# A Swin block and a dilated-convolution block on one core: the pyramid's matmuls spread evenly over four column tiles and reordered, the edge gate summed as rows and spread by a transfer

## The chip, the cores and the metric

The kernel runs on one core of one Trainium2 chip. The metric is the device time of one execution in microseconds (us); lower is better. All data are float32. An "image" below is one of 16 inputs of 128 channels by 32 x 32 points, held as 128 partitions x 1024 elements.

## The reference, cut to what matters

Two blocks follow each other for each image. The first is a Swin block (layer norm, attention in windows of 8 x 8 points with 8 heads, projection, layer norm, an MLP of 512 hidden channels). The second is a convolution block; the part of it that the change touches is this:

```python
out0 = gelu(conv2d(x, in_w, in_b))
feats = [conv2d(out0, pyr_w[i], pyr_b[i], pad=(d, d), dil=(d, d), groups=dim // 4)
         for i, d in enumerate((1, 6, 12, 20))]          # 3 x 3 taps, 32 outputs each
pyr = conv2d(conv2d(concatenate(feats), fuse_w, fuse_b, groups=dim), cr_w[2], cr_b[2], pad=(1, 1), groups=dim)
edge = sigmoid(conv2d(out0, vis_w, vis_b, pad=(1, 1)))   # one plane for all channels
out = x + cw0 * (1 + edge) * h_out + cw1 * (1 + edge) * v_out + cw2 * (1 - 0.3 * edge) * pyr + cw3 * point + cw4 * x_sca
```

`h_out` and `v_out` are dilated convolutions along one axis followed by 3 x 3 ones, and `x_sca` goes through a 2-D Fourier transform, a product and the inverse transform. Relu and a last 1 x 1 convolution close the block.

## The kernel before, in words

**Order of the work.** Each engine has a hand-written list of steps, and semaphores join them. The convolution block of image n runs beside the Swin block of image n + 1, in a function `both(n, i)` that every engine has; the queues run it 15 times, and `conv_only` handles the last image. Within `both` a front stretch (input convolution, layer norm, keys, queries, values) is followed by eight slots j = 0 to 7, one for each pair of attention windows, and then by a tail (projection, MLP, output convolution). In slot j TensorE issues `scores(j + 2)`, `conv_early(n, j)`, `prob_transposes(j)`, `conv_late(n, j)` and `values(j)`. VectorE does `bias_max(j + 2)` (L957 and L960), `row_sums(j)` (L964 and L966) and `conv_slot(n, j)`. GpSimd subtracts the maxima (`less_max`, L1666), and ScalarE takes the exponents (`exponent`, L1382) and copies the transposed probabilities (`prob_copy`, L1387). An engine works its list in order, so a step that waits holds up everything behind it.

**The front stretch on TensorE** is: `in_conv` (L607), `x_transposes`, `edge_products` (L628), two taps of the pyramid's first half, `gap_products` (L614, L615), five more taps, `n_transposes` (L459, which waits for the normalised rows `nT` of VectorE, L929), `mid_products` (L620, L621), `queries_keys` (L489, L494), `v` (L504), the last two taps, then `scores(0)` and `scores(1)` (L518). These two wait for `spread_keys` (L428), eight transfers that the SP queue issues once VectorE has written the keys `kC` (L949). Taps 0 to 4 of the pyramid's second half come behind the two scores, tap 5 in slot 0, and taps 6 to 8 in slot 1.

**The pyramid** (`pyramid`, L674) computes the four dilated 3 x 3 convolutions. The image's rows are split in two halves k of 16 rows; half k goes to PSUM bank 4 + k. Dilation d (1, 6, 12, 20) owns column tile d of the array, that is 32 output partitions, so up to four matmuls can run side by side, each with 128 rows and 32 columns. A tap reads a shifted rectangle, and points outside the image are left out. So tile 0 (dilation 1) takes 4,418 columns in each half, tile 1 takes 3,528, tile 2 takes 2,592 and tile 3 takes 1,568. In the profile each float32 matmul is two instructions. The second half waits for `route_z` and `xs_sb`, two signals of `scaled_input` on VectorE. ScalarE copies each half to `pyr` (`pyr_copy`, L1452), and `stack_pyramid` on the SP queue (L417) makes three shifted copies of it in `pyr_stack` with 12 transfers; `pyramid_conv` (L647, slot 5) reads them.

**The edge gate.** `edge_products` yields nine planes, one for each tap of the 3 x 3 filter. `spread_edge` on the SP queue writes them to DRAM and reads them back shifted, as nine partitions (`z_run`, L410). In slot 5, TensorE adds the nine and spreads the sum over all 128 partitions by a matmul with ones (`edge_spread`, L637, 2 x 512 columns, into banks 6 and 7), ScalarE takes two tanh of 128 x 512 (`edge_tanh`, L1437) and then the gate of the pyramid (`edge_cuts`, L1445), which VectorE's `gate_pyramid` (L1139, slot 6) waits for. `inverse_even` (slot 5, in the same banks, the first L467 group after VectorE's `even_product` L1117) waits for the tanh, and ScalarE's `inverse_even_copy` stands behind `edge_cuts` in its list.

**The Fourier part** goes back and forth between TensorE and ScalarE: `x2_conv` (slot 1), `dft_rows` and `turn_spectrum` (slot 2), `r_even` and `dft_columns` (slot 3), `r_odd` (slot 4). VectorE mirrors the input in slot 1 (`odd_part`), adds a bias in slot 3 (`r_even_bias`, L1099), boosts in slot 4 (`boosted`, L1108) and multiplies in slot 5. VectorE's share of the axis convolutions is 18 passes of 128 x 1024 (`taps`, L1088 and L1090); nine of them run in the tail, ahead of `gate_axes` (L1147), `add_magnitude` (L1153) and `mixture` (L1159), on which ScalarE's relu (L1521) and the output convolution (L755) wait.

## Time and profile before

| what | us |
|---|---|
| three runs, median (lowest, highest) | 1809.78 (1808.87, 1812.44) |
| the profiled execution, its own time | 1805.41 |
| span of the profiled execution | 1803.6 |
| TensorE, busy | 1549.4 |
| VectorE, busy | 1364.0 |
| ScalarE, busy | 864.2 |
| GpSimd, busy | 684.9 |

The span is one execution on the core as the profiler saw it, and what lies around it (1.8 us) is launch and end. Busy times are summed over the instructions of an engine, and they overlap between engines. TensorE is busiest by this count, but its matmuls are pipelined, and a busy engine need not be the one that sets the end; which one does is read from the chain of waits and from the timelines. The mean granted clock of TensorE is 0.953 of full speed.

### The profile page before, as it was taken

The page shows a single profiled execution, that of the slowest core. Times are in us where ns is not written, and L with a number is a line of the kernel's source. Part 1 is how long each engine was busy: PE and PEld are TensorE (multiplying, and loading weights), DVE is VectorE, ACT ScalarE, POOL GpSimd, SP SyncE. Part 2 cuts the span into 40 slices and gives each one's busy share as a digit, 9 for nine tenths or more (in the row PEclk, how much of TensorE's full clock was granted, in tenths as well). Part 3 has the DMA queues.
Part 4 walks back from the last instruction along what each step waited for, and adds up shares of the span by engine and source line. Part 5 has one row for each costly group of instructions (what it writes and reads, how often), then busy time and mean ns, then how long its engine had stood idle before and what let it go on. Part 6 is the DMA issues. An engine that isn't in the chain of part 4 may idle for free.

```text
span 1803.6 us, 32142 instructions
## 1 busy us (share of the span) xinstructions
PE 1549.4 (86%) x11664; PEld 906.3 (50%) x11664; DVE 1364.0 (76%) x2455; ACT 864.2 (48%) x1380; POOL 684.9 (38%) x603
## 2 busy tenths in 40 slices
PE   5789899888989889888998988889888898988884
PEld 3346455464555546445463554546455464555542
DVE  4558778687777878788687777868788786778866
ACT  2344545455454544545455454544545545454533
POOL 3244251634416244251534416134251623416151
PEclk9899999999999999999999999999999999999997
DMA  4011020111102011020111102011020201102020
GB/s 147 1 26 41 26 52 1 43 33 37 39 23 53 0 37 39 25 51 0 43 33 37 39 23 53 0 37 39 25 51 0 58 18 37 39 12 53 0 54 12
DMA packets 19618, 60.23 MB, mean 33 GB/s; under 512 B 6228, under 2 KB 6228, under 8 KB 19204
## 3 DMA queue, kind: packets, MB, share of 16 engines
q1 hardware_dynamic: 19588, 59.83, 13.7%
q8 instruction: 18, 0.29, 0.1%
q14 instruction: 12, 0.10, 0.0%
HBM read 14.04 MB, written 9.02 MB: 13 GB/s over the span
## 4 chain that ended last, share of the span: by engine, by line
DVE 39%; PE 25%; DVEq 16%; issue 7%; ACT 6%; SPq 4%; DMA 3%; ACTq 1%; POOL 0%; POOLq 0%
DVE hv L1090 16%; DVEq L959 7%; DVE nT L929 5%; PE bank L647 5%; PE bank L674 4%; SPq L428 4%; DVE row_max L960 4%; DVEq L965 3%; PE bank L467 3%; PE bank L518 3%; PE bank L489 2%; DMA k_heads<-kC 2%; PE bank L755 2%; DVE score L957 2%; PE bank L577 1%
## 5 line engine op out<-in xcount | busy, mean ns | idle before, releaser
L674 PE MATMUL bank<-act,mats_sb 128*32 128x512 f32 (+11 forms) x2112 | 267.1, 475 | 1.4 <-DVE xs L1026 1.4
L1666 POOL TENSOR_TENSOR score<-score,row_max 128x512 f32<-128x512 f32 x128 | 133.4, 1042 | 306.7 <-DVE row_max L960 305.1
L1350 ACT ACTIVATE fft<-bank 128x512 f32<-128x512 f32 x224 | 168.9, 807 | 125.7 <-PE bank L467 111.8
L1090 DVE SCALAR_TENSOR_TENSOR hv<-hor,mix,hv 128x1024 f32<-128x1024 f32 x128 | 193.8, 1514 | 10.7
L467 PE MATMUL bank<-cons_sb,fft 128*128 128x128 f32 x1280 | 185.4, 306 | 11.8 <-DVE fft L1117 11.8
L1090 DVE SCALAR_TENSOR_TENSOR hv<-ver,mix,hv 128x1024 f32<-128x1024 f32 x144 | 186.9, 1298 | 11.0
L1382 ACT ACTIVATE score<-score 128x512 f32<-128x512 f32 x128 | 80.8, 631 | 225.8 <-POOL score L1666 225.8
L467 PEld LDWEIGHTS bank<-cons_sb,fft 128*128 128x128 f32 x1280 | 172.7, 217 | 31.4 <-DVE fft L1117 17.0
L1677 POOL COPY inv_wide<-row_inv 128x128 f32<-128x128 f32 x128 | 91.8, 717 | 206.7 <-DVE row_inv L966 206.7
L674 PEld LDWEIGHTS bank<-act,mats_sb 128*32 128x32 f32 x2112 | 117.5, 109 | 99.6 <-issue 81.5
L1696 POOL TENSOR_SCALAR hor<-act,cols_sb 128x1024 f32<-128x1024 f32 x16 | 18.0, 1125 | 391.6 <-ACT act L1407 391.6
L518 PE MATMUL bank<-k_heads,qC 128*64 128x512 f32 x512 | 136.1, 621 | 31.8 <-DMA k_heads<-kC 31.8
L577 PE MATMUL bank<-nC,mats_sb 128*128 128x512 f32 x256 | 127.4, 621 | 38.9 <-ACT nC L1350 23.4
L957 DVE TENSOR_TENSOR score<-bank,rel_bias 128x512 f32<-128x512 f32 x128 | 87.2, 681 | 76.3 <-PE bank L518 76.2
L1387 ACT ACTIVATE probT<-bank 128x512 f32<-128x512 f32 x128 | 77.7, 607 | 101.6 <-PE bank L529 101.3
L1706 POOL TENSOR_SCALAR axis_part<-act,cols_sb 128x320 f32<-128x320 f32 (+1 forms) x128 | 109.4, 855 | 22.5 <-issue 22.5
L587 PE MATMUL bank<-fft,mats_sb 128*128 128x512 f32 x256 | 115.2, 593 | 0.0
L1400 ACT ACTIVATE fft<-bank,fold_b 128x512 f32<-128x512 f32 x128 | 79.2, 689 | 68.5 <-PE bank L577 68.5
L929 DVE TENSOR_SCALAR nT<-xT,mv,rstd 128x128 f32<-128x128 f32 x256 | 104.8, 491 | 3.8
L1708 POOL TENSOR_TENSOR ver<-ver,axis_part 128x320 f32<-128x320 f32 (+1 forms) x64 | 100.8, 1575 | 9.4
L960 DVE TENSOR_REDUCE row_max<-score 128x8 f32<-128x512 f32 x128 | 87.8, 686 | 11.6
L577 PEld LDWEIGHTS bank<-nC,mats_sb 128*128 128x128 f32 x256 | 45.1, 191 | 98.2 <-issue 34.4
(180 smaller groups left out, 2903.9 us busy)
## 6 DMA issues: line engine op xcount, KB each, us to landing
pyr_stack<-pyr SPq DMA_DIRECT2D x192, 144.2 KB, 3.1
x_in<-x_dram SPq DMA_DIRECT2D x16, 512.0 KB, 3.5
k_heads<-kC SPq DMA_DIRECT2D x128, 64.0 KB, 2.4
out_dram<-y_out SPq DMA_DIRECT2D x16, 512.0 KB, 2.8
k_heads<-rel_dram SPq DMA_DIRECT2D x2, 1024.0 KB, 13.0
mats_sb<-mats_dram SPq DMA_DIRECT2D x1, 1978.5 KB, 7.4
z_dram<-z_sb SPq DMA_DIRECT2D x32, 19.1 KB
z_run<-z_dram SPq DMA_DIRECT2D x16, 38.2 KB
```

The costliest lines, as they stand in the source:

```text
L467: last = pe.matmul(dst[:, c * P:(c + 1) * P], src[:, at:at + P], rhs, start=True, stop=True)
L518: last = pe.matmul(bank[2 + j % 2][64 * e:64 * e + 64, :], qC[:, w * WT:(w + 1) * WT], k_heads[:, :, w], start=True, stop=True)
L577: pe.matmul(bank[b][:], w_up[:, f * P:(f + 1) * P], nC[:, HALF * k:HALF * k + HALF], start=True, stop=True).then_inc(up_ps, 1)
L587: last = pe.matmul(bank[b][:], w_down[:, f * P:(f + 1) * P], hidden[:, f, HALF * k:HALF * k + HALF], start=False, stop=(f == FC - 1))
L674: last = pe.matmul(grids[32 * d:32 * d + 32, y0 - 16 * k:y1 - 16 * k, x0:x1], w_pyr[:, d, t], act[:, y0 + dy:y1 + dy, x0 + dx:x1 + dx], st ...
L929: last = dve.tensor_scalar(nT[:, c], source[:, c], mv[:, c, 0:1], rstd[:, c:c + 1], ALU.subtract, ALU.mult)
L957: dve.tensor_tensor(score[:, j % 3].rearrange("p h k -> p (h k)"), bank[2 + j % 2][:], rel_bias[:], ALU.add).then_inc(s_biased, 1)
L959: dve.drain()
L960: dve.tensor_reduce(row_max[:, j % 3], score[:, j % 3], AX.X, ALU.max).then_inc(s_max, 1)
L1090: last = dve.scalar_tensor_tensor(hv[:], src, mix[:, a, k:k + 1], hv[:], ALU.mult, ALU.add)
L1350: return act_.activation(dst, src, ACT.Copy)
L1666: pool.tensor_tensor(score[:, j % 3], score[:, j % 3], row_max[:, j % 3].unsqueeze(2).broadcast_to([P, HEADS, WT]), ALU.subtract)\
```

## The change: what it does

Five things change. The pyramid's dilation 1 keeps 12 rows of each half in tile 0; the other 8 rows of the image (24 to 31) go to tile 3, into partitions 96 to 127 of bank 7. A half then takes at most 3,528 columns in one tile: the tiles hold 3,290, 3,528, 2,592 and 2,696 columns in the first half and 3,384, 3,528, 2,592 and 2,602 in the second, in 42 matmuls each where there were 33. `pyramid_pieces` orders them by the columns that each tile has had so far. ScalarE gets a third copy (`rest_copy`, slot 1, ahead of the second `pyr_copy`), `stack_pyramid` issues 18 transfers, and the second half of `x2_conv` waits for the new copy, since it overwrites bank 7.

The second half no longer waits for `route_z` and `xs_sb`, and the taps are placed otherwise: three of the first half, `gap_products`, the other six and two of the second half ahead of `n_transposes`; three of the second half ahead of `scores(0)`; none behind `scores(1)`. Tap 5 and taps 6 to 8 stay in slots 0 and 1.

The edge planes are read back as rows (`z_rows`, 32 partitions, one for each row of the image) with three transfers; VectorE sums them in slot 1 (`sum_edge`, 32 x 32 out of 32 x 288); ScalarE takes one tanh of 32 x 32 in slot 2; and `widen_edge` on the SP queue, behind `stack_pyramid`, writes the 4 KB to DRAM and reads them into all 128 partitions. The matmul `edge_spread` is gone, `edge_cuts` and `gate_axes` wait for the transfer, and `inverse_even` waits for `boosted` in place of the tanh.

```diff
-                taps = bass.AP(z_dram, 0, [[3 * GRID1 + S1, 3], [GRID1 + 1, 3], [1, RUN]])
-                sp.dma_start(z_run[0:9, 0:RUN], taps).then_inc(z_in, 16)
+                for y in range(3):
+                    taps = bass.AP(z_dram, y * (3 * GRID1 + S1), [[S1, SIDE], [GRID1 + 1, 3], [1, SIDE]])
+                    sp.dma_start(z_rows[0:SIDE, 3 * y:3 * y + 3], taps).then_inc(z_in, 16)
+            def widen_edge(n):
+                sp.wait_ge(edge_tanhed, n + 1)
+                sp.dma_start(edge_dram[:], edge_rows[0:SIDE]).then_inc(edge_out, 16)
+                sp.wait_ge(edge_out, 16 * n + 16)
+                sp.dma_start(edge.rearrange("p h w -> p (h w)"), bass.AP(edge_dram, 0, [[0, P], [1, TOK]]))\
+                  .then_inc(edge_sb, 16)
             def stack_pyramid(n):
                 sp.wait_ge(pyr_sb, 2 * n + 2)
+                sp.wait_ge(rest_sb, n + 1)
+                flat = pyr.rearrange("p h w -> p (h w)")
+                rest = pyr_rest.rearrange("p h w -> p (h w)")
+                end = 33 * S1 + SIDE
+                low, high = (1 + MAIN1) * S1, (1 + 2 * MAIN1) * S1
                 for s in range(3):
-                    for j in range(4):
-                        src = pyr[32 * j:32 * j + 32].rearrange("p h w -> p (h w)")
-                        sp.dma_start(pyr_stack[32 * s:32 * s + 32, j, 0:33 * S1 + SIDE], src[:, s:s + 33 * S1 + SIDE])\
+                    part = slice(32 * s, 32 * s + 32)
+                    for j in range(1, 4):
+                        sp.dma_start(pyr_stack[part, j, 0:end], flat[32 * j:32 * j + 32, s:s + end])\
                           .then_inc(pyr_stacked, 16)
+                    sp.dma_start(pyr_stack[part, 0, 0:low - s], flat[0:32, s:low]).then_inc(pyr_stacked, 16)
+                    sp.dma_start(pyr_stack[part, 0, low - s:high - s], flat[0:32, 17 * S1:17 * S1 + high - low])\
+                      .then_inc(pyr_stacked, 16)
+                    sp.dma_start(pyr_stack[part, 0, high - s:end], rest[96:P, 0:end - high + s])\
+                      .then_inc(pyr_stacked, 16)
...
                 stack_pyramid(n)
+                widen_edge(n)
                 store(n)
...
                 return max(first, -off), min(first + count, SIDE - off)
+            def pyramid_pieces(k):
+                chains = [[(0, MAIN1 * k, MAIN1, t) for t in PYR_ORDER]]
+                chains += [[(d, 16 * k, 16, t) for t in PYR_ORDER] for d in range(1, 4)]
+                chains[3] += [(0, 2 * MAIN1 + REST1 // 2 * k, REST1 // 2, t) for t in PYR_ORDER]
+                pieces, busy = [], [0, 0, 0, 0]
+                while any(chains):
+                    tile = min((g for g in range(4) if chains[g]), key=lambda g: busy[g])
+                    d, first, count, t = chains[tile].pop(0)
+                    (y0, y1) = inside(first, count, (t // 3 - 1) * DILS[d])
+                    (x0, x1) = inside(0, SIDE, (t % 3 - 1) * DILS[d])
+                    if y1 > y0:
+                        pieces.append((tile, d, first, t, y0, y1, x0, x1, not chains[tile]))
+                        busy[tile] += max(64, (y1 - y0) * (x1 - x0))
+                return pieces
+            PYR_PIECES = [pyramid_pieces(k) for k in range(2)]
             def pyramid(n, k, steps):
                 pe.wait_ge(act_sb, 2 * n + 2)
                 if k == 0:
                     pe.wait_ge(out_sb, 2 * n)
-                else:
-                    pe.wait_ge(route_z, n + 1)
-                    pe.wait_ge(xs_sb, n + 1)
+                pieces = PYR_PIECES[k]
                 grids = bank[4 + k].rearrange("p (h w) -> p h w", w=SIDE)
-                for step in steps:
-                    t = PYR_ORDER[step]
-                    for d, dil in reversed(tuple(enumerate(DILS))):
-                        dy, dx = (t // 3 - 1) * dil, (t % 3 - 1) * dil
-                        (y0, y1), (x0, x1) = inside(16 * k, 16, dy), inside(0, SIDE, dx)
-                        if y1 > y0:
-                            last = pe.matmul(grids[32 * d:32 * d + 32, y0 - 16 * k:y1 - 16 * k, x0:x1], w_pyr[:, d, t],
-                                             act[:, y0 + dy:y1 + dy, x0 + dx:x1 + dx],
-                                             start=(step == 0), stop=(step == 8), skip_group_check=True)
-                    if step == 8:
+                rest = bank[7].rearrange("p (h w) -> p h w", w=SIDE)
+                for at in range(len(pieces) * steps[0] // 9, len(pieces) * (steps[-1] + 1) // 9):
+                    tile, d, first, t, y0, y1, x0, x1, final = pieces[at]
+                    dy, dx = (t // 3 - 1) * DILS[d], (t % 3 - 1) * DILS[d]
+                    if tile == d:
+                        to = grids[32 * d:32 * d + 32, y0 - first:y1 - first, x0:x1]
+                    else:
+                        to = rest[96:P, y0 - 2 * MAIN1:y1 - 2 * MAIN1, x0:x1]
+                    last = pe.matmul(to, w_pyr[:, d, t], act[:, y0 + dy:y1 + dy, x0 + dx:x1 + dx], start=(t == 4),
+                                     stop=(t == PYR_ORDER[8]), skip_group_check=True)
+                    if final:
                         last.then_inc(pyr_ps, 1)
...
                     pe.wait_ge(xs_sb, n + 1)
+                    if k == 1:
+                        pe.wait_ge(rest_sb, n + 1)
...
                     pe.wait_ge(ge_sb, n + 1)
-                    pe.wait_ge(edge_sb, 2 * n + k + 1)
+                    pe.wait_ge(w_sb, 2 * n + 2)
...
-                elif j == 5:
-                    edge_spread(n)
...
                 in_conv(n)
                 x_transposes(i)
                 edge_products(n)
-                pyramid(n, 0, range(0, 2))
+                pyramid(n, 0, range(0, 3))
                 gap_products(n)
-                pyramid(n, 0, range(2, 7))
+                pyramid(n, 0, range(3, 9))
+                pyramid(n, 1, range(0, 2))
                 n_transposes(i)
                 mid_products(n)
                 queries_keys(i)
                 v(i)
-                pyramid(n, 0, range(7, 9))
+                pyramid(n, 1, range(2, 5))
                 scores(i, 0)
                 scores(i, 1)
-                pyramid(n, 1, range(0, 5))
                 for j in range(PAIRS):
                     if j + 2 < PAIRS:
...
+            def sum_edge(n):
+                dve.wait_ge(z_in, 48 * n + 48)
+                dve.wait_ge(edge_tanhed, n)
+                dve.tensor_reduce(edge_sum[0:SIDE], z_rows[0:SIDE].rearrange("p t x -> p x t"), AX.X, ALU.add)\
+                   .then_inc(edge_summed, 1)
...
                 elif j == 1:
+                    sum_edge(n)
                     odd_part(n)
...
             def edge_tanh(n):
-                for k in range(2):
-                    act_.wait_ge(eb_ps, 2 * n + k + 1)
-                    act_.wait_ge(gated_sb, n)
-                    act_.activation(edge[:, 16 * k:16 * k + 16], bank[6 + k].rearrange("p (h w) -> p h w", w=SIDE),
-                                    ACT.Tanh, bias=half_vis_b[:], scale=0.5).then_inc(edge_sb, 1)
+                act_.wait_ge(edge_summed, n + 1)
+                act_.wait_ge(edge_out, 16 * n)
+                act_.activation(edge_rows[0:SIDE], edge_sum[0:SIDE], ACT.Tanh, bias=half_vis_b[0:SIDE], scale=0.5)\
+                    .then_inc(edge_tanhed, 1)
             def edge_cuts(n):
-                act_.drain()
+                act_.wait_ge(edge_sb, 16 * n + 16)
                 act_.wait_ge(axis_sb, 2 * n + 2)
                 act_.wait_ge(cw_sb, n + 1)
                 act_.activation(edge_cut[:], edge[:], ACT.Identity, bias=mix[:, 2, 1:2], scale=mix[:, 2, 0:1])\
                     .then_inc(cut_sb, 1)
             def pyr_copy(n, k):
-                act_.wait_ge(pyr_ps, 2 * n + k + 1)
-                act_.wait_ge(pyr_stacked, 16 * 12 * n)
+                act_.wait_ge(pyr_ps, 8 * n + 4 * k + 4)
+                act_.wait_ge(pyr_stacked, 16 * 18 * n)
                 act_.activation(pyr[:, 1 + 16 * k:17 + 16 * k, 1:1 + SIDE],
                                 bank[4 + k].rearrange("p (h w) -> p h w", w=SIDE), ACT.Identity, bias=fuse_bias[:],
                                 scale=col("fuse_w")).then_inc(pyr_sb, 1)
+            def rest_copy(n):
+                act_.wait_ge(pyr_ps, 8 * n + 8)
+                act_.wait_ge(pyr_stacked, 16 * 18 * n)
+                act_.activation(pyr_rest[96:P, 0:REST1, 1:1 + SIDE],
+                                bank[7][96:P, 0:REST1 * SIDE].rearrange("p (h w) -> p h w", w=SIDE), ACT.Identity,
+                                bias=rest_bias[96:P], scale=col("rest_w")[96:P]).then_inc(rest_sb, 1)
...
                 elif j == 2:
+                    edge_tanh(n)
                     row_spectrum_copy(n)
-                elif j == 5:
-                    edge_tanh(n)
...
             def conv_late(n, j):
                 if j == 1:
+                    rest_copy(n)
                     pyr_copy(n, 1)
                     x2_copy(n)
```

## Rows read from the trace of the kernel before

**Rows 1.** The page: busy time of PE, and the engines' shares of the chain.

```profile
PE 1549.4 (86%) x11664; PEld 906.3 (50%) x11664; DVE 1364.0 (76%) x2455; ACT 864.2 (48%) x1380; POOL 684.9 (38%) x603
...
DVE 39%; PE 25%; DVEq 16%; issue 7%; ACT 6%; SPq 4%; DMA 3%; ACTq 1%; POOL 0%; POOLq 0%
```

**Rows 2.** Timeline of PE, one image: start us, us, instructions, [idle before it <-releaser].

```profile
968.32 1.88 PE L607 MATMUL bank<-xm,mats_sb 128*128 128x512 f32 x4
...
974.81 4.27 PE L674 MATMUL bank<-act,mats_sb 128*32 128x480 f32 x34
...
981.54 0.66 PE L459 MATMUL bank<-cons_sb,nT 128*128 128x128 f32 x4 [1.80 <-DVE nT L929]
...
988.20 1.87 PE L674 MATMUL bank<-act,mats_sb 128*32 128x144 f32 x16
992.20 1.94 PE L518 MATMUL bank<-k_heads,qC 128*64 128x512 f32 x8 [2.13 <-DMA k_heads<-kC]
994.07 4.42 PE L674 MATMUL bank<-act,mats_sb 128*32 128x512 f32 x40
...
1002.16 2.62 PE L674 MATMUL bank<-act,mats_sb 128*32 128x128 f32 x20
...
1013.06 1.08 PE L518 MATMUL bank<-k_heads,qC 128*64 128x512 f32 x4
```

**Rows 3.** Timeline of DVE, same image and columns.

```profile
999.54 0.69 DVE L957 TENSOR_TENSOR score<-bank,rel_bias 128x512 f32<-128x512 f32 x1 [2.13 <-PE bank L518]
...
1001.80 0.11 DVE L1064 TENSOR_REDUCE vec<-route 128x1 f32<-128x5 f32 x1
...
1015.64 0.68 DVE L957 TENSOR_TENSOR score<-bank,rel_bias 128x512 f32<-128x512 f32 x1
...
1023.25 0.68 DVE L964 TENSOR_REDUCE row_sum<-score 128x8 f32<-128x512 f32 x1
...
1028.11 1.34 DVE L1117 TENSOR_TENSOR fft<-fft 128x1024 f32<-128x1024 f32 x1
...
1038.41 0.75 DVE L1139 SCALAR_TENSOR_TENSOR py<-bank,cols_sb,axis_part 128x512 f32<-128x512 f32 x1 [1.73 <-PE bank L647]
```

**Rows 4.** Timeline of ACT, same image and columns.

```profile
988.29 0.21 ACT L1427 ACTIVATE route<-route 128x5 f32<-128x5 f32 x1
...
1000.12 0.60 ACT L1387 ACTIVATE probT<-bank 128x512 f32<-128x512 f32 x1
...
1029.23 1.24 ACT L1445 ACTIVATE axis_part<-edge,mix 128x1024 f32<-128x1024 f32 x1
```

**Rows 5.** Timeline of PE around slot 5, same image and columns as Rows 2.

```profile
1025.90 1.97 PE L637 MATMUL bank<-z_run,ones 9*128 9x512 f32 x4 [0.99 <-DVE fft L1113]
...
1029.50 3.55 PE L467 MATMUL bank<-cons_sb,fft 128*128 128x128 f32 x16 [1.04 <-DVE fft L1117]
```

**Rows 6.** Timeline of SP, same image: the first issue's start, us, issues.

```profile
1006.69 7.50 SPq L417 DMA_DIRECT2D pyr_stack<-pyr  x12
```

**Rows 7.** The page, DMA issues: count, KB each, median us from issue to landing.

```profile
x_in<-x_dram SPq DMA_DIRECT2D x16, 512.0 KB, 3.5
...
k_heads<-rel_dram SPq DMA_DIRECT2D x2, 1024.0 KB, 13.0
```

**Rows 8.** Timeline of PE, where later images' in_conv begins, same columns.

```profile
1074.99 0.59 PE L607 MATMUL bank<-xm,mats_sb 128*128 128x512 f32 x1
...
1182.89 1.45 PE L607 MATMUL bank<-xm,mats_sb 128*128 128x512 f32 x3
...
1292.57 1.88 PE L607 MATMUL bank<-xm,mats_sb 128*128 128x512 f32 x4
...
1399.23 1.88 PE L607 MATMUL bank<-xm,mats_sb 128*128 128x512 f32 x4
```

**Rows 9.** Windows: from:to us, us, busy (x) by engine, PEclk, DMA share, GB/s.

```profile
1029.40:1036.20 6.80, 6.70 (x48) 4.43 (x52) 3.69 (x7) 3.65 (x4) 0.49 (x2) 0.76 0.00 0
...
1196.60:1203.40 6.80, 6.80 (x13) 3.42 (x12) 2.72 (x5) 0.94 (x2) 6.17 (x7) 0.50 0.02 2
```

More of the change, by code:

```diff
@@ L48 @@
 GRID1 = S1 * S1
-RUN = 31 * S1 + SIDE
+MAIN1 = 12
+REST1 = SIDE - 2 * MAIN1
 AXIS_DIL, AXIS_TAPS = 11, 7
@@ L315, in swin_conv_kernel @@
         z_in = sem("z_in")
-        eb_ps = sem("eb_ps")
+        edge_summed = sem("edge_summed")
+        edge_tanhed = sem("edge_tanhed")
+        edge_out = sem("edge_out")
         edge_sb = sem("edge_sb")
@@ L319, in swin_conv_kernel @@
         pyr_sb = sem("pyr_sb")
+        rest_sb = sem("rest_sb")
         pyr_stacked = sem("pyr_stacked")
@@ L445, in _ @@
             stack_pyramid(IMAGES - 2)
+            widen_edge(IMAGES - 2)
             store(IMAGES - 2)
@@ L448, in _ @@
             stack_pyramid(IMAGES - 1)
+            widen_edge(IMAGES - 1)
             store(IMAGES - 1)
@@ L630, in edge_products @@
                 last.then_inc(z_ps, 1)
-            def edge_spread(n):
-                pe.wait_ge(w_sb, 2 * n + 2)
-                pe.wait_ge(z_in, 16 * n + 16)
-                for k in range(2):
-                    pe.matmul(bank[6 + k][:], ones[0:9], z_grid[0:9, 16 * k:16 * k + 16, 0:SIDE], start=True,
-                              stop=True).then_inc(eb_ps, 1)
             def pyramid_conv(n):
                 pe.wait_ge(go_sb, 2 * n + 2)
-                pe.wait_ge(pyr_stacked, 16 * 12 * n + 16 * 12)
+                pe.wait_ge(pyr_stacked, 16 * 18 * n + 16 * 18)
                 for k in range(2):
@@ L1284, in _ @@
             dve.tensor_scalar(fuse_bias[:], col("pyr_b"), col("fuse_w"), col("fuse_b"), ALU.mult, ALU.add)
+            dve.tensor_scalar(rest_bias[:], col("rest_pyr_b"), col("rest_w"), col("rest_b"), ALU.mult, ALU.add)
             dve.tensor_scalar(two_b1[:], row("fgm_b1"), 2.0, None, ALU.mult)
@@ L1433, in edge_tanh @@
             def edge_tanh(n):
-                for k in range(2):
-                    act_.wait_ge(eb_ps, 2 * n + k + 1)
-                    act_.wait_ge(gated_sb, n)
-                    act_.activation(edge[:, 16 * k:16 * k + 16], bank[6 + k].rearrange("p (h w) -> p h w", w=SIDE),
-                                    ACT.Tanh, bias=half_vis_b[:], scale=0.5).then_inc(edge_sb, 1)
+                act_.wait_ge(edge_summed, n + 1)
+                act_.wait_ge(edge_out, 16 * n)
+                act_.activation(edge_rows[0:SIDE], edge_sum[0:SIDE], ACT.Tanh, bias=half_vis_b[0:SIDE], scale=0.5)\
+                    .then_inc(edge_tanhed, 1)
             def edge_cuts(n):
-                act_.drain()
+                act_.wait_ge(edge_sb, 16 * n + 16)
                 act_.wait_ge(axis_sb, 2 * n + 2)
@@ L1641, in _ @@
             pool.sem_inc(z_zeroed, 1)
-            for padded in (hor, ver, pyr):
+            for padded in (hor, ver, pyr, pyr_rest):
                 pool.memset(padded[:], 0.0)
@@ L1798 @@
     put("pyr_b", conv["pyr_b"].reshape(-1))
+    for name, of in (("rest_w", "fuse_w"), ("rest_pyr_b", "pyr_b"), ("rest_b", "fuse_b")):
+        cols[96:P, COLS[name][0]] = conv[of].reshape(-1)[:32]
     put("vis_b", np.repeat(conv["vis_b"], P))
```

12 lines of the change are left out of this document (8 added, 4 removed).

## The prediction

> **What bounds the kernel now.** I read the page first, then the chain, then the timelines of one image. The page puts PE at 1549.4 us of busy time, but the chain that ended last lies on DVE and its queue for 55% and on PE for 25% [rows 1]: DVE sets the end, and PE counts where DVE waits for it. The timelines say where. In the image from 968.32 to 1074.99, DVE has one long wait for PE ahead of the slots, 2.13 us at 999.54 [rows 2, 3]. PE was running five taps of the pyramid's second half then (4.42 us from 994.07), with the scores that DVE wanted queued behind them [rows 2]. DVE then runs almost without a gap to `even_product` at 1028.11, waits in slot 6 for `pyramid_conv` (1.73 us for the second half, which begins at 1038.41), and is busy again to the tail's end [rows 3]. PE has holes of its own: 1.80 us before the second `n_transposes` and 2.13 us before `scores(0)`, where it waits for the transfer of the keys [rows 2].
>
> **Cost of a column.** The 20 matmuls of 994.07 load tile 0 most, with 2,512 columns. At 1.667 ns a column (four cycles of 2.4 GHz) that is 4.19 us, and 0.23 us of start and end give the 4.42 of the row. The three taps at 1002.16 (1,441 columns in tile 0) give 2.40 + 0.22 = 2.62, again the row [rows 2]. So a stretch of pyramid costs the columns of its fullest tile, and the other tiles run free beside it.
>
> A rule of the Trainium skill speaks against this: TensorE: Matmul & The Clock Gate, Part 3 (The mechanism), says that matmuls start and end strictly in program order. Started so, each when its tile is free and the one before it has begun, the 20 matmuls would take 7.2 us by my count from their columns. The row has 4.42, so this trace does not agree; by the row the sum below is 1789, by the rule it would be the last but one of the rivals, 1889.
>
> **The change, part by part, in that image.**
>
> 1. *Ahead of `n_transposes`.* Before, seven taps load tile 0 with 3,426 columns. Afterwards three taps (1,120 in the fullest tile), `gap_products`, and the other six with two of the second half (3,364, tile 1) make 4,484: 1,058 more, 1.76 us. The hole behind the first transposes is 1.80 us [rows 2], so this just fits, at no cost. `gap_products` comes 143 columns (0.24 us) later, and DVE still waits for ScalarE's standard deviation after it: nothing. Were that cover short, each tenth of a us here would move the keys and everything behind them.
> 2. *Ahead of `scores(0)`.* Three taps with 1,152 columns take 1.92 + 0.22 = 2.14 us, where 1.87 stood; the hole of 2.13 behind them takes the 0.27 [rows 2]. Cost nothing. The two old waits are long met there.
> 3. *Behind `scores(1)`.* The 4.42 us go. `scores(2)` can start when bank 2 is read, at about 994.1, and is done 1.08 later [rows 2]. DVE is free at 999.54 - 2.13 = 997.41, so its wait shrinks to about 0.07: **2.06 us** earlier [rows 3]. From here PE idles until ScalarE's `prob_copy(0)` at 1000.12, which waits for DVE, GpSimd and the exponent and does not move [rows 4].
> 4. *Slot 1.* The last taps cost 1,256 columns, 2.31 us, for 2.62 [rows 2]. But `x2_conv`'s second half waits for `rest_copy`, which ScalarE begins after `prob_copy(1)`. Its cost lies between a copy of 128x5 (0.21) and one of 128x512 (0.60) [rows 4]; I take 0.45 for 32x256. This gives back the 0.3, so `scores(5)` ends where it did, 1013.06 + 1.08 = 1014.14 [rows 2].
> 5. *`sum_edge` on DVE.* 288 elements a partition, between the reduction of five (0.11) and of 512 (0.68) [rows 3]: 0.4. `z_in` is long there: SP issues the three reads well before the keys. The small tanh on ScalarE in slot 2 costs about 0.21 [rows 4] and is over before `dft_rows` has a result for it to copy: nothing.
> 6. *What is late next.* DVE would begin `bias_max(5)` 2.06 - 0.4 = 1.66 us earlier than 1015.64 [rows 3], at 1013.98, and finds the scores done at 1014.14 and a signal behind them: 1014.24, a gain of **1.4 us**. The chain behind it (`r_even_bias`, `r_odd`, `scores(7)`, `boosted`) hangs on DVE, and `even_product` comes 1.4 us earlier. PE's work from there to the tail is unchanged, so PE and DVE both move by 1.4.
> 7. *`edge_spread` gone.* 1.97 us of PE [rows 5], in a stretch where PE waits for `even_product` anyway (1.04 more behind it): nothing gained, and the wait before `inverse_even` grows to over 3 us.
> 8. *The edge transfer.* SP starts `stack_pyramid` where it did (1006.69). 18 issues at 7.50 / 12 = 0.63 us end at 1018.0 [rows 6]. Then 0.63 and about 2.5 for the 4 KB (under the 3.5 that 512 KB need), 0.63 and 3.5 for the 512 KB [rows 7] put `edge` there at 1025.3. ScalarE comes to `edge_cuts` at about 1029.23 - 1.4 - 1.97 = 1025.9 [rows 4, 5], needs 1.24 for it, and must then be free for `inverse_even`'s first copy near 1029. Cost nothing, with 2 us in hand. The stacked copies land by about 1021.5, long before `pyramid_conv`. Behind them SP has only the store, which waits for the image's end.
>
> **The clock.** Images come in a cycle of three: 107.90, 109.68 and 106.66 us [rows 8]. In the 109.68 one the granted clock is 0.50, half of 2.4 GHz, from 1196.6 to 1203.4, just behind the 1.8 us hole and across keys and queries [rows 9]. That image is 1.8 us longer than its neighbour, and there are five such among 15. The new taps fill the hole, so I take this drop as gone: -9. In every image the clock also falls before `inverse_even` (0.76 over 1029.4 to 1036.2 [rows 9]); its 16 instructions take 3.55 us [rows 5]. The idle time ahead of it grows, and I add 0.2 us an image: +3. And the new idle stretch from 995.3 to 1000.8, broken by one group of transposes and one tap, lies before taps, `x2_conv` and `scores(5)`. A drop there would cost PE half of some 3 us and eat the 1.4: I count it for a third of the images, +7.
>
> **Sum.** 15 x 1.4 = 21; the last image gains 1 (its pyramid runs 1.5 us shorter ahead of `mid_products`, less `sum_edge`), and the larger setup nothing that shows. -21 - 1 - 9 + 3 + 7 = -21 us: 1805.4 for the profiled execution's own time becomes 1784.4. The median of the runs is 4.4 us above that execution, so I forecast 1784.4 + 4.4 = **1789** (-1.2%). A measurement can tell 0.2%, about 3.6 us.
>
> **The rivals.**
>
> - *The clock holds too.* No new drop, and the copy's wait shorter so that DVE keeps 1.66: -25 - 1 - 9 + 0 = -35, 1775. For it: one short stretch of work breaks the idle time. Chance 0.12.
> - *The clock falls in the emptied stretch in most images (no change).* For it: the idle time is longer than the hole that preceded the drop at 1196.6 [rows 9]. A drop of 3.3 us (0.76 over 6.8 us is half clock for that long) costs PE 1.7 before `scores(5)`, 0.3 more than the gain: +4.5 - 9 + 3 - 1, about 1807. Chance 0.12.
> - *Slower: the same drop, twice as long, every image.* The drop at 1196.6 lasted 6.8 us [rows 9]; 3.4 us lost ahead of `scores(5)` is 2.0 beyond the gain. It decides from the point where `scores(5)` ends over 1.4 us later. 15 x 2.0 - 9 + 3 - 1 = +23, 1833. Against it: PE works solidly from 1000.8 on. Chance 0.08.
> - *The edge is late.* Two broadcasts of 1 MB took 13.0 us each [rows 7]. At 13 us `edge` lands at 1035, ScalarE holds `inverse_even`'s copies until then, but `turn_even` wants them only near 1040, and `gate_pyramid` loses some 0.8 us: +12, 1801. Chance 0.06.
> - *Program order.* If the tiles did wait for one another, the uneven pieces ahead of `n_transposes` would take 14.2 us, 6.7 more than summed, and 15 x 5.3 us would make it about 1889. That is the skill's rule of above. The trace bears it out nowhere. Chance 0.02.
> - *The forecast's own case*, 1778 to 1800: chance 0.60.
>
> **How the numbers follow.** Faster by over 0.2%: 0.60 + 0.12 + 0.06 and 0.03 of the case at 1807, that is 0.81. Within 0.2%: the rest of that case less its upper edge, 0.08. Slower: 0.11. The range 1772 to 1807 leaves out the slower cases and half of the one at 1807.
>
> **What would show it.** Right: no wait of DVE for L518 before `bias_max(2)`; the pyramid's busy time down by 14 to 20%; images of some 105.5 us with no clock of 0.50 in the keys. Step 6 is wrong if DVE waits more than 0.3 us at `bias_max(5)`, step 1 if `n_transposes` starts late without waiting for DVE, step 8 if ScalarE waits over 3 us for the transfer. The forecast falls if the granted clock is 0.50 between slots 0 and 2 in most images.

## The result and the profile after

The changed kernel takes 1827.07 us (median of four runs, 1826.86 to 1828.2). The kernel before took 1811.11 us beside it (four runs, 1808.87 to 1814.13). The ratio on record is 1.0074, 95% interval 1.0047 to 1.0101 (the two medians alone give 1.0088): slower, where 1789 was forecast with a range to 1807. The profiled execution took 1827.1 us (span 1825.3). Before's took 1805.4, less than any of its four runs, so the two traces differ by 21.7 us of span and the medians by 16. The mean granted clock fell from 0.953 to 0.928.

From the page after: busy time of the engines (PE is TensorE, PEld its weight loads, DVE VectorE, ACT ScalarE, POOL GpSimd), the shares of the chain, the pyramid's group, and the edge's transfer. Beside it stands [rows 1]; the last line is the pyramid's group on the page before.

```profile
PE 1507.9 (83%) x12176; PEld 928.0 (51%) x12176; DVE 1368.7 (75%) x2472; ACT 847.3 (46%) x1380; POOL 702.2 (38%) x604
...
DVE 39%; PE 28%; ACT 9%; DVEq 8%; issue 8%; SPq 4%; DMA 3%; POOL 1%; ACTq 1%; POOLq 0%
...
L712 PE MATMUL bank<-act,mats_sb 128*32 128x512 f32 (+13 forms) x2688 | 243.0, 436 | 0.0
...
edge<-edge_dram SPq DMA_DIRECT2D x16, 512.0 KB, 3.6
```

```profile
L674 PE MATMUL bank<-act,mats_sb 128*32 128x512 f32 (+11 forms) x2112 | 267.1, 475 | 1.4 <-DVE xs L1026 1.4
```

PE is busy 41.5 us less than before, and the kernel is slower. So the time is not in the amount of work. The pyramid's busy time fell by 9%, where 14 to 20% were forecast; part of its taps now run at half speed, as shown below.

Where the images begin says which part of the program it is in. By line, `in_conv` after: duration least/median/most, first and last start.

```profile
L636 PE MATMUL bank<-xm,mats_sb x64: 592/592/697, 107.8 to 1747.7; 128*128 128x512 f32 x64
```

The same line before:

```profile
L607 PE MATMUL bank<-xm,mats_sb x64: 592/592/697, 101.9 to 1724.8; 128*128 128x512 f32 x64
```

First to last start is 1639.9 us after and 1622.9 before, **+17.0**. The last start is that of the sixteenth image's fourth instruction, 1.3 us behind its first, in both; so fifteen images take (1639.9 - 1.3) / 15 = 109.2 us each instead of 108.1. Ahead of the first image it is 107.8 for 101.9, **+5.9**. The last image takes 1825.3 - 1746.4 = 78.9 for 80.1, **-1.2**. Together 21.7.

PE's timeline of the image from 1091.12 to 1200.32; it answers to [rows 2, 5].

```profile
1091.12 1.88 PE L636 MATMUL bank<-xm,mats_sb 128*128 128x512 f32 x4
...
1097.81 5.89 PE L712 MATMUL bank<-act,mats_sb 128*32 128x341 f32 x71
1103.62 1.40 PE L488 MATMUL bank<-cons_sb,nT 128*128 128x128 f32 x8
...
1111.02 2.13 PE L712 MATMUL bank<-act,mats_sb 128*32 128x384 f32 x28
1114.96 2.95 PE L547 MATMUL bank<-k_heads,qC 128*64 128x512 f32 x12 [1.80 <-DMA k_heads<-kC]
1119.49 0.65 PE L558 MATMUL bank<-cons_sb,score 128*128 128x128 f32 x4 [1.58 <-ACT score L1428]
1120.08 0.89 PE L712 MATMUL bank<-act,mats_sb 128*32 128x416 f32 x10
1123.39 0.66 PE L569 MATMUL bank<-probT,v_pair 128*32 128x64 f32 x16 [2.43 <-ACT probT L1433]
1123.98 1.98 PE L547 MATMUL bank<-k_heads,qC 128*64 128x512 f32 x4
1125.89 3.62 PE L712 MATMUL bank<-act,mats_sb 128*32 128x124 f32 x28
...
1131.45 1.13 PE L496 MATMUL bank<-mats_sb,xs 128*128 128x128 f32 x8 [0.47 <-ACT pyr_rest L1506]
...
1138.48 1.08 PE L547 MATMUL bank<-k_heads,qC 128*64 128x512 f32 x4
...
1153.47 3.78 PE L496 MATMUL bank<-cons_sb,fft 128*128 128x128 f32 x16 [4.00 <-DVE fft L1161]
1157.18 6.30 PE L668 MATMUL bank<-pyr_stack,mats_sb 96*32 96x512 f32 x48
```

The front is as the steps wanted it: both `n_transposes` in one go at 1103.62, three taps in 2.13 us, `scores(0)` to `scores(2)` without a break. These twelve instructions end at 1117.91. Behind them stand two holes, 1.58 and 2.43 us, with `prob_transposes(0)` and one tap between. What follows runs at half speed: the four instructions of `scores(3)` at 1123.98 take 1.98 us, and 1.08 at 1138.48; those of `values(0)` ahead of them take 0.66 us, and 0.43 behind a filled hole (`fill_slot0` below).

Windows after, with the columns of [rows 9]:

```profile
1104.60:1111.00 6.40, 6.40 (x80) 4.13 (x78) 4.18 (x6) 3.46 (x5) 5.77 (x7) 1.00 0.19 29
1121.60:1128.40 6.80, 5.01 (x43) 2.78 (x45) 6.33 (x11) 2.23 (x4) 6.11 (x5) 0.50 0.00 0
1152.30:1159.10 6.80, 5.63 (x28) 4.08 (x32) 4.48 (x6) 2.56 (x3) 1.55 (x3) 0.50 0.00 0
```

The front's drop of [rows 9] is gone (keys and queries at 1.00). But the granted clock is 1.2 GHz for 6.8 us from 1121.6, inside the second hole, and for 6.8 us from 1152.3, inside the 4.00 us wait ahead of `inverse_even`. The same two stand about 30.5 and 61.2 us into every image but the last. So the images no longer come in a cycle of three [rows 8]: each takes 109.1 to 109.3 us, one 109.7.

DVE's timeline of that image, beside [rows 3]:

```profile
1120.09 0.68 DVE L994 TENSOR_TENSOR score<-bank,rel_bias 128x512 f32<-128x512 f32 x1
...
1129.03 0.64 DVE L1116 TENSOR_REDUCE edge_sum<-z_rows 32x32 f32<-32x288 f32 x1
...
1134.00 0.69 DVE L994 TENSOR_TENSOR score<-bank,rel_bias 128x512 f32<-128x512 f32 x1 [2.23 <-PE bank L547]
1139.60 0.69 DVE L994 TENSOR_TENSOR score<-bank,rel_bias 128x512 f32<-128x512 f32 x1 [0.78 <-PE bank L547]
...
1152.07 1.34 DVE L1161 TENSOR_TENSOR fft<-fft 128x1024 f32<-128x1024 f32 x1
```

`bias_max(2)` at 1120.09 has no wait left; it comes 28.97 us into the image instead of 31.22. Later DVE gives this back and more: it waits 2.23 us for `scores(4)` and 0.78 for `scores(5)`. Position in the image:

| | before | forecast | after |
|---|---|---|---|
| `scores(5)` done | 45.82 | 45.82 | 48.44 |
| `bias_max(5)` begins | 47.32 | 45.92 | 48.48 |
| `even_product` begins | 59.79 | 58.4 | 60.95 |

### The profile page after: what moved, and what is told of

It reads as the page before. It is cut to its first block, busy times and chain, and to the rows that moved or that the text cites. A ratio compares the mean times of both kernels' runs of the same rounds, so it can differ in the third digit from the quotient of the medians.

```text
span 1825.3 us, 33365 instructions
## 1 busy us (share of the span) xinstructions
PE 1507.9 (83%) x12176; PEld 928.0 (51%) x12176; DVE 1368.7 (75%) x2472; ACT 847.3 (46%) x1380; POOL 702.2 (38%) x604
## 4 chain that ended last, share of the span: by engine, by line
DVE 39%; PE 28%; ACT 9%; DVEq 8%; issue 8%; SPq 4%; DMA 3%; POOL 1%; ACTq 1%; POOLq 0%
DVE hv L1134 17%; PE bank L668 5%; DVE nT L966 5%; PE bank L496 5%; PE bank L547 5%; SPq L454 4%; PE bank L712 3%; DVE row_max L997 3%; DVEq L996 2%; DMA k_heads<-kC 2%; DVEq L1002 2%; PE bank L794 2%; DVE score L994 2%; PE bank L518 2%; ACT fft L1396 2%
## 5 line engine op out<-in xcount | busy, mean ns | idle before, releaser
L712 PE MATMUL bank<-act,mats_sb 128*32 128x512 f32 (+13 forms) x2688 | 243.0, 436 | 0.0
L712 PEld LDWEIGHTS bank<-act,mats_sb 128*32 128x32 f32 x2688 | 149.5, 117 | 70.7 <-issue 54.0
L1731 POOL COPY inv_wide<-row_inv 128x128 f32<-128x128 f32 x128 | 95.9, 750 | 216.8 <-DVE row_inv L1003 216.8
L547 PE MATMUL bank<-k_heads,qC 128*64 128x512 f32 x512 | 150.3, 684 | 30.7 <-DMA k_heads<-kC 30.7
L966 DVE TENSOR_SCALAR nT<-xT,mv,rstd 128x128 f32<-128x128 f32 x256 | 105.1, 493 | 3.8
L558 PE MATMUL bank<-cons_sb,score 128*128 128x128 f32 x512 | 82.4, 284 | 24.0 <-ACT score L1428 24.0
L668 PE MATMUL bank<-pyr_stack,mats_sb 96*32 96x512 f32 x768 | 100.3, 676 | 0.0
```

What stands on the lines that cost most here:

```text
L547: last = pe.matmul(bank[2 + j % 2][64 * e:64 * e + 64, :], qC[:, w * WT:(w + 1) * WT], k_heads[:, :, w], start=True, stop=True)
L668: last = pe.matmul(bank[4 + k][32 * j:32 * j + 32, :], w_stack[0:96, y, j], runs, start=(y == 0), stop=(y == 2))
L712: last = pe.matmul(to, w_pyr[:, d, t], act[:, y0 + dy:y1 + dy, x0 + dx:x1 + dx], start=(t == 4), stop=(t == PYR_ORDER[8]), skip_group_chec ...
L966: last = dve.tensor_scalar(nT[:, c], source[:, c], mv[:, c, 0:1], rstd[:, c:c + 1], ALU.subtract, ALU.mult)
```

## The experiments

**Theory:** the holes left behind `scores(2)` bring 6.8 us at half clock across slots 0 and 1 of every image, and that is the whole loss; without it the steps hold. **Rivals:** the uneven pyramid itself (its pieces, or its copies) delays the stage; or the edge part does (its reduction on DVE, or PE idle where `edge_spread` was). Where "unread matmuls" are added, they multiply two constants into bank 6, and nothing reads the result.

**Matmuls into the hole.** After, with one unread matmul behind `scores(2)` and two behind tap 5, both in slot 0:

```
+def fill(n, count, done, level):
+    pe.wait_ge(done, level)
+    for c in range(count):
+        pe.matmul(bank[6][:], mat("fgm2"), mats_sb[:, 0:HALF], start=True, stop=True)
 conv_late, j == 0:
     pyramid(n, 1, range(5, 6))
+    fill(n, 2, xs_sb, n + 1)
 both, behind scores(i, j + 2):
+    if j == 0:
+        fill(n, 1, xs_sb, n + 1)
```

> The kernel after, with three more matmuls of 128x512 whose results nothing reads, in TensorE's idle time: one behind scores(2), two behind tap 5 in slot 0. They add work and remove none. Theory (clock): the drop of the granted clock that begins 30.5 us into every image goes, TensorE's stretch to scores(5) gets back its 2.6 us, VectorE keeps 1.4 us against the kernel before, and an image takes about 106.6 us instead of 109.2: 1827 - 39 = 1788 us, and no window of 0.50 between slots 0 and 2. Rival (the clock is a by-product; rest_copy's wait, the sum on VectorE and the late scores would cost the same at full clock): 1825 to 1835 us, images of 109 us or more, since only work was added.

1774.28 us (1770.67 to 1778.45), ratio to before 0.9797 (0.9765 to 0.983). Its image starts at 951.88. PE timeline, the first two rows being the added matmuls (two instructions each), and two windows:

```profile
978.56 1.12 PE L801 MATMUL bank<-mats_sb 128*128 128x512 f32 x2
...
981.62 1.98 PE L801 MATMUL bank<-mats_sb 128*128 128x512 f32 x4
...
984.48 1.08 PE L547 MATMUL bank<-k_heads,qC 128*64 128x512 f32 x4
985.49 2.43 PE L712 MATMUL bank<-act,mats_sb 128*32 128x124 f32 x28
```

```profile
982.40:989.20 6.80, 6.28 (x63) 3.43 (x61) 6.33 (x11) 2.79 (x6) 6.19 (x5) 1.00 0.00 0
1012.20:1015.60 3.40, 3.40 (x20) 3.17 (x22) 3.11 (x5) 1.16 (x2) 0.00 (x0) 0.50 0.00 0
```

With all the work of the changed kernel, its uneven pieces and its third copy among it, plus three matmuls an image, the kernel is 53 us faster than after, and 14 below what was expected. At the place of the drop the clock is 1.00: `scores(3)` takes 1.08 for 1.98, the taps 2.43 for 3.62, and `scores(5)` ends 46.10 us into the image for 48.44. The second drop is half as long. The images take 105.8 us (105.3 to 106.1).

**The same without added work.** After, with tap 5 moved from slot 0's end to its beginning, and taps 6 to 8 from slot 1 into slot 0:

```
 conv_early: 
-    if j == 1:
-        pyramid(n, 1, range(6, 9))
+    if j == 0:
+        pyramid(n, 1, range(5, 6))
 conv_late, j == 0:
-    pyramid(n, 1, range(5, 6))
+    pyramid(n, 1, range(6, 9))
```

> The kernel after, with the pyramid's tap 5 moved from behind to ahead of prob_transposes(0), and taps 6 to 8 from slot 1 into slot 0, so that real work lies in the idle stretch. Theory (clock): as many columns in the stretch keep the clock up; x2_conv and scores(5) come up to 2.3 us earlier, VectorE no longer waits at bias_max(5): images of about 106 us, 1780 us. Rival (no clock effect): the 2.3 us of taps leave slot 1 all the same and scores(5) gains up to 2.3 us of the 2.6 that it lost, so time falls too, but the granted clock still shows 0.50 in slots 0 to 2: about 1795 us.

1771.34 us (1769.56 to 1772.58), ratio 0.9775 (0.9748 to 0.9803). Its image starts at 951.39; windows and PE timeline:

```profile
974.00:1008.00 34.00, 27.18 (x252) 16.41 (x252) 30.73 (x52) 15.47 (x26) 18.46 (x17) 1.00 0.28 70
1008.90:1015.70 6.80, 5.14 (x24) 3.89 (x28) 4.89 (x7) 2.38 (x3) 2.05 (x3) 0.50 0.00 0
```

```profile
1010.56 3.79 PE L496 MATMUL bank<-cons_sb,fft 128*128 128x128 f32 x16 [4.01 <-DVE fft L1161]
1014.28 6.04 PE L668 MATMUL bank<-pyr_stack,mats_sb 96*32 96x512 f32 x48
```

The clock stays at 1.00 over all the slots up to the wait for `even_product`, and falls only there. `bias_max(5)` begins at +45.32 without a wait. 105.8 us an image again: the place of four taps, not their number, was worth 56 us. The rival, in which the clock stays at 0.50 and the earlier taps bring about 1795, fell.

**The two parts apart.** The edge part alone, on the kernel before:

```
-        z_run = sb("z_run", 32 * S1)
+        z_rows = sb("z_rows", 9, SIDE)
...
+    def widen_edge(n):
...
-    elif j == 5:
-        edge_spread(n)
+    sum_edge(n)
```

> The kernel before with the edge part of the change alone (planes read as rows, summed on VectorE, tanh of 32x32, spread by a transfer; no edge_spread matmul). Theory (clock): it leaves slots 0 to 2 as before, adds 0.6 us of VectorE to each image and 2 us of idle TensorE ahead of inverse_even, where the clock fell already: 0.6 x 16 = +10 us, up to +20 if the drop there is always the long one: 1820 to 1830 us. Rival (the edge part is free and all the loss is the pyramid's): within 4 us of the kernel before.

1815.71 us (ten runs, 1811.65 to 1822.03), ratio 1.0018 (1.0002 to 1.0034). The 10 to 20 us that were expected of the edge part did not come; the rival (within 4 us of before) held. The images still vary (106.9 to 109.7 us). In this one trace the front's drop stands at its full 6.8 us in eight of them, where before's trace has five, and their mean is 108.8 us for 108.1. That need not be the edge part's doing: before's own executions differ among themselves (thirteen of them took 1806.32 to 1816.13 us, with a mean granted clock of 0.945 to 0.954). DVE's reduction:

```profile
1011.92 0.65 DVE L1084 TENSOR_REDUCE edge_sum<-z_rows 32x32 f32<-32x288 f32 x1
```

The pyramid part alone (after, with these same lines undone):

> The kernel after with the edge part undone (the matmul edge_spread and the two tanh are back): the pyramid's part of the change alone. Theory (clock): the drop from 30.5 us on stays, 0.6 us of VectorE go, and scores(5) decides, so little is won: 1818 to 1827 us. Rival (the edge transfer makes the loss): back to 1790 or less.

1830.21 us (1829.49 to 1832.54), ratio 1.0108 (1.008 to 1.0136). The same place, 30.5 us into its image:

```profile
1009.00:1015.80 6.80, 4.91 (x43) 2.78 (x45) 6.33 (x12) 2.33 (x4) 6.08 (x4) 0.50 0.00 0
```

Images of 109.2 us with both drops, as after: inside the images the slowdown is the pyramid part's. The total lies above the 1818 to 1827 expected, and the excess comes from the last image, which takes 84.5 us here, 78.9 after and 80.1 before. So the pyramid part alone loses 4.4 us there and the edge part with it gains 5.6; the edge part by itself (79.3) gained 0.8. The clock is in this too: in the last image it is at 0.50 for 13.7 us from 30.4 us on here, and for 3.4 us after. `r_odd`, `edge_spread` and `inverse_even` lie in it and take 3.75, 3.78 and 3.78 us; the kernel before, whose clock holds there, needs 2.02, 1.98 and 2.02.

**The edge part, once the drop is gone.** The taps moved as above, with the edge part undone:

> The run taps_slot0 with the edge part of the change undone (the matmul edge_spread and two tanh in slot 5 are back). VectorE has 0.6 us less in slot 1, TensorE 2 us more ahead of inverse_even. Theory (the edge part costs a bit more than it gives): 1762 to 1771 us. Rival (once the clock holds, the edge part pays its 2 us of TensorE): 1785 us or more.

1775.36 us (1773.75 to 1777.67), ratio 0.9788 (0.9749 to 0.9827): above the theory's 1762 to 1771, and far from the rival's 1785. All images but the first take 105.6 to 105.9 us, as with the new edge. So `edge_spread` was hidden, and its removal neither costs nor gains inside an image. The last image takes 84.5 us for 78.7, with the 13.7 us drop of the pyramid part alone; in the trace an earlier start (103.0 for 105.4) and shorter first images take 4 of these 6 us back.

**Is it the hole or the slot?** After, with taps 2 to 4 moved from ahead of `scores(0)` to behind `scores(1)`, so that the last hole is filled and the wait for the keys bare:

```
 both:
-    pyramid(n, 1, range(2, 5))
     scores(i, 0)
     scores(i, 1)
+    pyramid(n, 1, range(2, 5))
```

> The kernel after, with the three taps of the second half (2.13 us) put back behind scores(1): the tiles stay even and the waits stay away, only the place is the old one. TensorE's hole ahead of scores(0) grows from 1.8 to 3.9 us, and the one behind them shrinks. VectorE needs scores(2) 3.6 us behind scores(1) and loses nothing. Theory (clock): the stretch behind the scores is full again, so the drop at 30.5 us goes, but one may come behind the longer hole ahead of scores(0): about 1775 without it, 1800 to 1815 with it. Rival (the old place itself costs the 2 us of VectorE as in the kernel before, whatever the clock): about 1805 with no drop in the clock.

1797.47 us (1797.1 to 1799.41), ratio 0.9904 (0.9874 to 0.9934). PE timeline and window:

```profile
989.31 3.68 PE L547 MATMUL bank<-k_heads,qC 128*64 128x512 f32 x8 [3.81 <-DMA k_heads<-kC]
992.92 3.00 PE L712 MATMUL bank<-act,mats_sb 128*32 128x384 f32 x28
```

```profile
987.90:994.70 6.80, 5.39 (x23) 2.24 (x27) 4.37 (x9) 0.77 (x3) 2.08 (x2) 0.50 0.07 12
```

The drop went with the idle time. It now begins within the 3.81 us hole, and `scores(0)`, `scores(1)` and the taps pay. Images alternate between 108.3 us and 106.7, with 6.8 and 3.4 us at half clock there. The time is just under the 1800 to 1815 that were expected if a drop came behind the longer hole; the rival, in which the old place costs its 2 us with no drop in the clock, fell.

**The second drop.** The good order, with three unread matmuls ahead of `inverse_even`, released when DVE has read the banks:

```
 conv_late, j == 5:
+    fill(n, 3, w_sb, 2 * n + 2)
     inverse_even(n)
```

> The run taps_slot0 with three added matmuls of 128x512 (results unread) between boosted and inverse_even, in TensorE's idle 4.0 us of slot 5. Theory (clock): inverse_even's 16 instructions fall from 3.79 to 2.05 us and pyramid_conv from 6.04 to 5.36, so an image is up to 2.4 us shorter and the kernel runs at about 1771 - 36 = 1735 us. Rival (VectorE sets the end there, and the drop before inverse_even is hidden): no change from 1771.

**1737.62 us** (1734.87 to 1738.62), ratio 0.9573 (0.9536 to 0.9611). Its image starts at 931.81; PE timeline, and the image as one window:

```profile
987.36 2.84 PE L801 MATMUL bank<-mats_sb 128*128 128x512 f32 x6 [0.33 <-DVE fft L1164]
...
991.04 2.05 PE L496 MATMUL bank<-cons_sb,fft 128*128 128x128 f32 x16 [0.84 <-DVE fft L1168]
993.02 5.36 PE L668 MATMUL bank<-pyr_stack,mats_sb 96*32 96x512 f32 x48
```

```profile
931.80:1035.20 103.40, 90.58 (x761) 55.09 (x760) 85.11 (x152) 52.84 (x87) 43.05 (x37) 1.00 0.16 38
```

The whole image runs at 2.4 GHz, in 103.4 us; of the fifteen, two have a drop of 3.4 us, 88 us in. `inverse_even` takes 2.05 for 3.79, `pyramid_conv` 5.36 for 6.04. This is the best kernel of the study, 4.3% faster than before and 4.9% faster than after.

Both fillings, in after's own order (the first and this one):

> The run fill_slot0 (the kernel after, three unread matmuls in the idle time of slots -1 and 0) with three more ahead of inverse_even. Theory (clock): 1774 - 30 = about 1744 us or a little less, with no window of 0.50 from the front stretch to the tail in most images. Rival: no change from 1774, since only work was added.

1749.98 us (1747.96 to 1753.58), ratio 0.9641 (0.9604 to 0.9679), most images 104.2 us: 6 us above the 1744 expected. The moved taps do better than the added matmuls in slot 0.

**The front's drop alone.** Before, with one unread matmul in the 1.80 us hole between the two `n_transposes` [rows 2]:

```
 n_transposes, ahead of k == 0's four:
+    pe.wait_ge(mid_sb, n + 1)
+    pe.matmul(bank[6][:], mat("fgm2"), mats_sb[:, 0:HALF], start=True, stop=True)
```

> The kernel before, with one added matmul of 128x512 (result unread, 0.86 us for its two instructions) in the 1.8 us hole between the two n_transposes. Theory (clock): the drop behind this hole, in every third image, goes, and with it the images of 109.7 us: five times 1.8, 1813 - 9 = about 1804 us; the drop ahead of inverse_even stays in every image. Rival (the cycle of three has another cause): 1813 us, 109.7 us images still there.

1811.82 us (ten runs, 1807.4 to 1818.24), ratio 0.9988 (0.9968 to 1.0007), where about 1804 was expected: a miss. Timeline and window of the image from 1187.46, behind the next hole (the wait for the keys):

```profile
1211.33 3.63 PE L521 MATMUL bank<-k_heads,qC 128*64 128x512 f32 x8 [2.12 <-DMA k_heads<-kC]
```

```profile
1211.40:1214.80 3.40, 3.40 (x8) 0.69 (x8) 1.38 (x3) 0.00 (x0) 0.00 (x0) 0.50 0.00 0
```

The hole shrank to 0.94 us and the keys and queries run at 1.00, but every third image has its drop 23.9 us in, for 3.4 us, and takes 109.45 us for 109.7. There it strikes `scores(0)` and `scores(1)`, which take 3.63 us for 1.94 [rows 2]. The drop was moved, not removed.

**The setup.** The best kernel, with two unread matmuls for each pair of windows in the first Swin block, which runs alone ahead of the first image:

```
 swin_rest, for j in range(PAIRS):
+    pe.matmul(bank[6][:], mat("fgm2"), mats_sb[:, 0:HALF], start=True, stop=True)
     prob_transposes(i, j)
+    pe.matmul(bank[6][:], mat("fgm2"), mats_sb[:, 0:HALF], start=True, stop=True)
     values(i, j)
```

> The run taps_slot0_fill5 with two unread matmuls of 128x512 for each of the eight pairs of windows of the first Swin block, which runs alone and waits on its chain of exponents. Theory (clock): the half clock between 46 and 87 us goes, the first convolution begins 2 to 5 us earlier: about 1734 us. Rival (the waits there hide the clock, and the added matmuls only stand in the way): 1738 us or more.

1743.24 us (1741.51 to 1743.77), ratio 0.9607 (0.9567 to 0.9647): 5.6 us slower than without. Windows over the block, here and then in the best kernel:

```profile
46.00:87.30 41.30, 35.83 (x261) 16.97 (x262) 23.65 (x58) 13.37 (x22) 10.35 (x16) 0.97 0.00 1
```

```profile
46.00:87.30 41.30, 29.89 (x229) 16.37 (x226) 23.65 (x57) 13.01 (x21) 10.34 (x16) 0.71 0.00 1
```

The clock rose from 0.71 to 0.97, and yet the first `in_conv` came at 109.1 us instead of 105.1. PE's timeline here shows two of the added matmuls:

```profile
57.53 1.12 PE L846 MATMUL bank<-mats_sb 128*128 128x512 f32 x2
...
58.93 1.02 PE L848 MATMUL bank<-mats_sb 128*128 128x512 f32 x2
```

The chain that ended last runs through them. From 46 to 85 us, TensorE's pieces of the chain make 23.9 us in the best kernel. Here they make 25.7, of which twelve of the sixteen added matmuls are 11.3, so that 14.3 are left for the work itself. The clock was worth something there, and the added matmuls took it back: the block's last transposes begin at 84.70 us instead of 85.39. Then the clock falls from 85.0 us on for 6.8 us, in the block's MLP, which the chain runs through (six instructions in 5.46 us from 86.40, 2.81 in the best kernel). The 2 to 5 us that were expected did not come, but what a filling would do that stands only where TensorE waits is not shown.

## Why the prediction was wrong

**What failed** is the term of "The clock" that counted a drop in the emptied stretch "for a third of the images, +7". It came in fifteen of sixteen images, 6.8 us long. The right case was the rival "the same drop, twice as long, every image", priced at 1833 and given a chance of 0.08. Its deciding point was `scores(5)` later by over 1.4 us: it was 2.6. With the same work and the stretch filled, the images take 105.8 us for 109.2: with what it brings at the second drop, the term was worth 3.4 x 15 = 51 us where +7 stood. That the rival's 1833 lies near 1827 is in part luck: its sum is +23, and the trace's 21.7 hold 5.9 of the setup, which it had at nothing. The prediction's own sign of failure, a clock of 0.50 between slots 0 and 2 in most images, came true. What spoke against it, that PE works solidly behind the holes, was no protection: that solid work is what ran at half clock. The third of the images came from [rows 8, 9], where the front's drop stands in every third image. That was the habit of another, smaller hole; nothing tied its frequency to the new stretch. The stretch has two holes with 4.0 us of idle time against 1.80, which was reason to price a drop in all images among the first cases, not among the last.

**Step 1 was right**: `n_transposes` in one go, and the front's drop gone (1.00 from 1104.6). **Step 2 was right**: 2.13 us for 2.14, hole 1.80. Fourteen uneven matmuls (28 instructions), 1,152 columns in the fullest tile, take 2.13 us, the sum by the fullest tile. Started strictly in program order, each instruction when its tile is free and the one before it has begun, they would take 3.6 us by their columns (an estimate). So the rule of the Trainium skill (TensorE: Matmul & The Clock Gate, Part 3, The mechanism) that matmuls start and end in program order disagrees with the trace once more. The program order rival fell.

**Step 3 was right in size and wrong in worth.** `bias_max(2)` came 2.25 us earlier (2.06 forecast). But the 4.42 us that went had also stood in what is now idle time, and with that stretch filled again the clock holds (the two orders above). In the two kernels of the first two experiments, which keep the clock there, the images take 105.8 us. The sum without the +7 gives before's 108.1 less 1.4, less 9 / 15, plus 0.2: 106.3. So the dependences were read rightly, and the clock undid them.

**Step 4**: `rest_copy` took 0.56 us (0.45 taken), and `x2_conv` waits 0.47 for it: small. "`scores(5)` ends where it did" holds to 0.3 us with the clock at 1.00 (+46.10 against +45.82), and fails by 2.6 without. **Step 5**: the reduction 0.64 for 0.4. **Step 6** was to be wrong if DVE waited over 0.3 us at `bias_max(5)`: it waited 0.78, and instead of 1.4 us gained, 1.16 were lost there. Step 6 itself needed nothing new; its input was late.

**Step 7 was half right.** Nothing was lost by the missing 1.97 us in the image (taps moved, with old and new edge: 105.8 each). The wait grew to 4.00. But the +0.2 us for the clock before `inverse_even` was too small: its instructions took 3.78 us and those of `pyramid_conv` 6.30, against 3.55 and 5.36 before, 1.17 more together. The 6.8 us at half clock now fall in every image, where before some had 6.8 and every third 3.4. That drop is not the edge part's, since the pyramid part alone has it too. Why it lasts 6.8 us with the taps moved and 3.4 with matmuls added in slot 0, at the same length of the images, is open; in both, `pyramid_conv` ends 68.9 to 69.0 us into the image. **Step 8 was right**. SP's timeline after, and ACT's:

```profile
1145.09 0.34 SPq L425 DMA_DIRECT2D edge<-edge_dram  x1
```

```profile
1130.75 0.56 ACT L1506 ACTIVATE pyr_rest<-bank,rest_bias,cols_sb 32x256 f32<-32x256 f32 x1
...
1149.99 1.23 ACT L1491 ACTIVATE axis_part<-edge,mix 128x1024 f32<-128x1024 f32 x1
```

The transfer issued at 1145.09 lands 3.6 us later (the page's row above), 57.6 us into the image (57.0 forecast), and `edge_cuts` begins at 1149.99 without a wait. The first of ACT's rows is step 4's `rest_copy`.

**Sum over an image.** +1.16 at `even_product` and +1.17 in the two groups behind it make 2.3 of the 2.5 us by which the image of 109.20 exceeds the one of 106.66 that the steps were worked in. Against the mean of the cycle it is 1.1, hence +17.0 over fifteen. The last image gained 1.2 for 1 forecast.

**The setup** was forecast at "nothing that shows", and lost 5.9 us. Mean clock over its last stretch, the kernel before and then after:

```profile
60.00:87.30 27.30, 19.29 (x150) 13.01 (x150) 14.70 (x45) 8.23 (x14) 4.41 (x8) 0.75 0.00 1
```

```profile
60.00:87.30 27.30, 19.79 (x152) 13.43 (x148) 14.21 (x37) 8.25 (x14) 5.69 (x10) 0.63 0.00 1
```

Part of it can be placed. Up to 84.1 us the setup of after and that of the best kernel agree to 0.01 us; then after's clock is at 0.50 until 87.3 and for 3.4 us from 94.2, and its first `in_conv` comes 2.7 us later (107.8 for 105.1). The two kernels have the same code there, so these 2.7 us come from where the drops fell. What of the other 3.2 belongs to the change stays open. The first `in_conv` starts at 102.3 us with the edge part alone, 105.6 with the pyramid part alone, 104.2 to 105.9 in five kernels that have both with taps moved or matmuls added in the images, and 107.8 after.

## What to carry to other kernels

Before work is taken out of a stretch in which TensorE waits soon after, ask what the granted clock will do behind every hole that the edit leaves, and price the half-clock case first: here it was the whole sign of the result. If an engine must wait anyway, put its movable work where the wait is, not around it; four taps moved by a slot or less were worth 56 us of 1827. And when a drop is removed, look for the next hole: it may only have moved.
